# Four transformer layers between two graph convolutions: the ends of a layer rearranged

## The reference

```python
h = _gcn(batch_norm(relu(layernorm(x))), src, dst, gcn_in_w, gcn_in_b, n)
for i in range(L):                                  # L = 4
    a = _attn(_ln(h, ln2_w[i], ln2_b[i]), cond, Wq[i], Wk[i], Wv[i], Wo[i])
    h = h + a
    u = _ln(h, ln3_w[i], ln3_b[i]) @ geglu_w[i] + geglu_b[i]
    val, gate = jnp.split(u, 2, axis=-1)
    f = val * jax.nn.gelu(gate, approximate=False)
    h = h + f @ ffo_w[i] + ffo_b[i]
h = _gcn(h, src, dst, gcn_out_w, gcn_out_b, n)
return h + x_in
```

## Time and profile before

| | |
|---|---|
| median of 3 executions | 2628.73 us (2624.0 to 2635.95) |
| the profiled execution | 2636.97 us, its span 2635.2 us |
| mean granted clock of PE | 0.971 |
| PE busy | 2516.3 us, 95% of the span |
| DVE, ACT, POOL busy | 52%, 38%, 25% |
| first convolution | to 252 us |
| layers 1 to 4 | from 251.6, 828.4, 1405.2 and 1982 us, some 576.8 us each (windows; the last to 2557) |
| second convolution | the last 78 us |
| chain that ended last | PE 87%, DVE 7%, ACT 2%, issue 2% |
| loads of `stage` | 138 pieces of 512 KB, 3.3 us to landing; 32 cond groups of 1 MB, 4.8 us |

### The profile page before, as it was taken

How to read it: one execution, slowest core, us unless ns; L and a number is a source line. 1 busy time by engine, 2 the same in 40 slices (tenths; PEclk the granted TensorE clock), 3 DMA queues, 4 the chain that set the end, 5 groups by cost and what they waited for, 6 DMA issues and landing times.

```text
span 2635.2 us, 35448 instructions
## 1 busy us (share of the span) xinstructions
PE 2516.3 (95%) x12535; PEld 2077.5 (79%) x12535; DVE 1378.5 (52%) x2834; ACT 1002.0 (38%) x1956; POOL 648.7 (25%) x492
## 2 busy tenths in 40 slices
PE   5868999999999999999999999999999999999999
PEld 2517788888887888888887888888887888888877
DVE  8996676642224667632225676622235676522235
ACT  8524444352222433452222444442223434532230
POOL 3000000044442000154441000254440000254431
PEclk7879999999999999999999999999999999999999
DMA  2002000012120000011110000021110000021120
GB/s 104 1 16 100 33 33 16 33 41 73 64 68 33 33 32 32 17 65 65 66 65 34 32 17 32 33 65 64 64 63 23 33 32 32 17 80 64 65 99 33
DMA packets 30658, 123.05 MB, mean 47 GB/s; under 512 B 3136, under 2 KB 3520, under 8 KB 26048
## 3 DMA queue, kind: packets, MB, share of 16 engines
q1 hardware_dynamic: 30528, 121.36, 13.4%
HBM read 115.05 MB, written 6.29 MB: 46 GB/s over the span
## 4 chain that ended last, share of the span: by engine, by line
PE 87%; DVE 7%; ACT 2%; issue 2%; POOL 1%; DMA 1%; POOLq 0%; DVEq 0%; ACTq 0%; SPq 0%
PE ps L1377 26%; PE ps L1378 26%; PE ps L1379 26%; PE ps L1559 2%; PE ps L1576 2%; PE ps L1578 2%; PE ps L1573 1%; DVE oh_d L1068 1%; DVE oh_s L1066 1%; DVE z L1274 1%; PE ps L1600 1%; PE ps L1586 1%; ACT oh_d L613 1%; PE ps L1481 0%; PE ps L1614 0%
## 5 line engine op out<-in xcount | busy, mean ns | idle before, releaser
L1377 PE MATMUL ps<-xT_hi,wg_hi 128*128 128x512 f32 (+1 forms) x1088 | 416.8, 383 | 0.0
L1379 PE MATMUL ps<-xT_hi,wg_lo 128*128 128x512 f32 (+1 forms) x1088 | 415.1, 382 | 0.0
L1378 PE MATMUL ps<-xT_lo,wg_hi 128*128 128x512 f32 (+1 forms) x1088 | 414.9, 381 | 0.0
L1327 DVE SCALAR_TENSOR_TENSOR ff<-ps,cols_sb,gel 128x512 f32<-128x512 f32 x128 | 96.1, 751 | 593.9 <-ACT gel L823 593.9
L823 ACT ACTIVATE gel<-ps,cols_sb 128x512 f32<-128x512 f32 x128 | 88.2, 689 | 638.0 <-PE ps L1379 638.0
L1336 DVE TENSOR_TENSOR h<-h,ps 128x512 f32<-128x512 f32 x256 | 175.2, 687 | 139.8 <-PE ps L1379 139.8
L1378 PEld LDWEIGHTS ps<-xT_lo,wg_hi 128*128 128x128 f32 x1088 | 209.8, 193 | 37.5
L1379 PEld LDWEIGHTS ps<-xT_hi,wg_lo 128*128 128x128 f32 x1088 | 209.9, 193 | 37.3
L1377 PEld LDWEIGHTS ps<-xT_hi,wg_hi 128*128 128x128 f32 x1088 | 210.0, 193 | 37.1
L400 POOL TENSOR_SCALAR veps<-mv 128x1 f32<-128x1 f32 x64 | 14.0, 219 | 819.1 <-DVE mv L889 819.1
L1377 PE MATMUL ps<-w_hi,cond_hi 128*128 128x512 f32 x512 | 204.0, 398 | 8.2 <-DVE cond_lo L998 6.9
(11 more groups left out here) (240 smaller groups left out, 5414.2 us busy)
## 6 DMA issues: line engine op xcount, KB each, us to landing
stage<-in_pieces SPq DMA_DIRECT2D x138, 512.0 KB, 3.3
stage<-in_condT SPq DMA_DIRECT2D x32, 1024.0 KB, 4.8
x<-in_x SPq DMA_DIRECT2D x2, 1024.0 KB, 6.7
res_s<-x SPq DMA_DIRECT2D x2, 1024.0 KB, 4.2
at_s<-at SPq DMA_DIRECT2D x1, 2048.0 KB, 9.9
at16b<-at_s SPq DMA_DIRECT2D x1, 2048.0 KB, 7.6
out<-h SPq DMA_DIRECT2D x8, 256.0 KB, 2.0
bias_row<-in_rows SPq DMA_DIRECT2D x6, 256.0 KB, 3.6
```

Source lines behind the costliest of these rows:

```text
L1327: dve.scalar_tensor_tensor(ff[:, s % 2, :], ps[:, step_bank(j, a, s, 0), :], cols_sb[:, bass.ds(COL["geglu_b"] + 32 * l + 4 * j + 2 * a + ...
L1377: pe.matmul(bank, l_hi, r_hi, start=(first and i == 0), stop=False)
L1378: pe.matmul(bank, l_hi, r_lo, start=False, stop=False)
L1379: end = pe.matmul(bank, l_lo, r_hi, start=False, stop=(last and i == n - 1))
```

## The change

What moves, by place:

- **Statistics and z2 of a layer's first tile** are made at the end of the layer before (the statistics after the second of the last eight additions to h, z2 after the last), before DVE's branch. z2 goes to a place of its own, `z2_first` (over `o_full`). For the first layer both stand inside and after the first convolution's `gcn(0)`.
- **cond group 1** is loaded right after cond group 0, at the end of the layer before, and split at the very beginning of a layer: ACT and DVE do it before anything else there.
- **First products** on PE: V 0, t2, V 1, Q, K 0, Q's transposes, V 2, S 0; the fourth V product goes into unit 0. x2's low part of group 0 is made by DVE.
- **Weight parts.** The low parts of the MLP's first two pieces go from POOL to DVE, behind unit 1's and inside unit 2's work of the last group.
- **Bias row.** The eight additions of the bias row to h leave `z3_of` and stand before the second, third and fourth ff of the MLP (2, 3 and 3 tiles).
- **Last transposes.** t3(7) stands one half-width product later. x3's low part of tile 7 goes to DVE; POOL's are done in two halves.
- Smaller: PE enters the first layer after three tiles of h instead of eight (`gcn_ok`), ACT waits for `agg_mm` before its loop.

```diff
@@ -332,10 +334,12 @@
+            sp.wait_ge(c_lo, 2)
+            load_raw(1)
...
             with sp.Fori(0, L) as l:
-                with sp.Fori(1, GROUPS) as g:
+                with sp.Fori(2, GROUPS) as g:
@@ -354,6 +358,8 @@
                 load_raw(0)
+                wait_apart(sp, c_lo, 2 * GROUPS * l + 2 * GROUPS + 2)
+                load_raw(1)
@@ -459,8 +466,6 @@
-                rsqrt(norm0)
-                x2_low(0)
@@ -472,9 +477,11 @@
                     pool.wait_ge(x3_hi_ok, NT * l + t + 1)
-                    pool.tensor_tensor(xT3_lo[t // 4][:, :, r],
-                                       full[:, t % 2, :].rearrange("p (k n) -> p k n", n=P),
-                                       bits(xT3_hi[t // 4][:, :, r]), ALU.subtract).then_inc(x3_ok, 1)
+                    for ks in (slice(0, 2), slice(2, KC)):
+                        last = pool.tensor_tensor(xT3_lo[t // 4][:, ks, r],
+                                                  full[:, t % 2, :].rearrange("p (k n) -> p k n", n=P)[:, ks, :],
+                                                  bits(xT3_hi[t // 4][:, ks, r]), ALU.subtract)
+                    last.then_inc(x3_ok, 1)
@@ -500,15 +507,11 @@
                 x3_low(1)
-                for r in range(2):
-                    w_low(FIRST_PIECES + PIECES * l + r, r, up_place(0, 0, r), up_place(1, 0, r))
-                    if r == 0:
-                        rsqrt(norm0 + 2 * NT - 2)
+                rsqrt(norm0 + 2 * NT - 2)
...
                 weights_low(0, 0, 0)
-                x3_low(7)
@@ -522,6 +525,7 @@
                 zero_q()
+                rsqrt(norm0 + 2 * NT)
@@ -794,20 +799,19 @@
-                for mc in range(2):
-                    v_high(UNITS * l + mc, mc, 0, V_BANK + mc)
-                x2_high(GROUPS * l)
-                v_high(UNITS * l + 2, 2, 0, V_BANK + 2)
-                k_high(UNITS * l)
-                q_copy(GROUPS * l)
-                act.wait_ge(qb_zero, 2 * l + 2)
-                q_high(GROUPS * l)
-                v_high(UNITS * l + 3, 3, 0, V_BANK + 3)
-                unit(UNITS * l, GROUPS * l, 0, 0, first=True)
...
                     cond_high(1, 1, part, stage)
+                v_high(UNITS * l, 0, 0, V_BANK)
+                x2_high(GROUPS * l)
+                v_high(UNITS * l + 1, 1, 0, V_BANK + 1)
+                q_copy(GROUPS * l)
+                k_high(UNITS * l)
+                act.wait_ge(qb_zero, 2 * l + 2)
+                q_high(GROUPS * l)
+                v_high(UNITS * l + 2, 2, 0, V_BANK + 2)
+                unit(UNITS * l, GROUPS * l, 0, 0, first=True)
@@ -1154,6 +1158,9 @@
                                              ALU.mult, ALU.add).then_inc(gcn_ok, 1)
+                    if not use and t == 1:
+                        dve.wait_ge(gcn_ok, 1)
+                        norm_stats(0, [h[:, 0, :]])
@@ -1162,8 +1169,15 @@
+            def z2_of(g, k, place=z2):
+                norm_wait(k)
+                dve.tensor_scalar(place[:, :], h[:, g, :], mv[:, 0:1], rstd[:, 0:1],
+                                  ALU.subtract, ALU.mult).then_inc(z2_ok, 1)
...
             dve.wait_ge(gcn_ok, NT)
+            z2_of(0, 0, z2_first)
@@ -1244,12 +1258,14 @@
                         o_part(u - 1, (p + 3) % 4)
-                    if not (last and p >= 1 or first):
+                    if not (last and p >= 1):
...
                         o_low(g - 1)
+                    if p == 2 and last:
+                        up_low(1)
                     if ln2:
-                        z2_of(t + 1, 1 if first else 2 * t)
+                        z2_of(t + 1, norm0 + (1 if first else 2 * t))
@@ -1260,6 +1276,8 @@
                         x2_full(g + 1)
+                    if p == 1 and last:
+                        up_low(0)
@@ -1273,13 +1291,32 @@
                                       ALU.subtract, ALU.mult).then_inc(z3_ok, 1)
-                    dve.wait_ge(z3_ok, GROUPS * l + g + 1)
-                    dve.tensor_tensor(h[:, g, :], h[:, g, :], bias_row[:, :], ALU.add).then_inc(h_bias, 1)
-                def z2_of(g, k):
-                    norm_wait(norm0 + k)
-                    dve.tensor_scalar(z2[:, :], h[:, g, :], mv[:, 0:1], rstd[:, 0:1],
-                                      ALU.subtract, ALU.mult).then_inc(z2_ok, 1)
+                def add_bias(tiles):
+                    for t in tiles:
+                        dve.tensor_tensor(h[:, t, :], h[:, t, :], bias_row[:, :], ALU.add).then_inc(h_bias, 1)
+                def up_low(r):
+                    n = FIRST_PIECES + PIECES * l + r
+                    wait_apart(dve, w_hi_ok, n + 1)
+                    dve.tensor_tensor(up_place(1, 0, r), stage[:, r, :], bits(up_place(0, 0, r)), ALU.subtract)\
+                        .then_inc(w_ok, 1)
+                def x2_low(g):
+                    dve.wait_ge(x2_hi_ok, g + 1)
+                    dve.tensor_tensor(xT2_lo[:, :, :].rearrange("p k n -> p (k n)"), full[:, 0, :],
+                                      bits(xT2_hi[:, :, :].rearrange("p k n -> p (k n)")),
+                                      ALU.subtract).then_inc(x2_ok, 1)
+                def x3_low(t):
+                    r = slice(t % 4 * P, (t % 4 + 1) * P)
+                    wait_apart(dve, x3_hi_ok, NT * l + t + 1)
+                    wait_apart(dve, x3_ok, 2 + NT * l + t)
+                    dve.tensor_tensor(xT3_lo[t // 4][:, :, r], full[:, t % 2, :].rearrange("p (k n) -> p k n", n=P),
+                                      bits(xT3_hi[t // 4][:, :, r]), ALU.subtract).then_inc(x3_ok, 1)
@@ -1295,21 +1332,17 @@
-                norm_stats(norm0, [h[:, 0, :]])
-                z2_of(0, 0)
-                for mc in range(2):
-                    v_low(UNITS * l + mc, mc, 0, V_BANK + mc)
+                for part in range(2):
+                    cond_low(GROUPS * l + 1, 1, part, stage)
                 x2_full(GROUPS * l)
-                v_low(UNITS * l + 2, 2, 0, V_BANK + 2)
+                v_low(UNITS * l, 0, 0, V_BANK)
+                x2_low(GROUPS * l)
+                v_low(UNITS * l + 1, 1, 0, V_BANK + 1)
...
                 q_low(GROUPS * l)
-                v_low(UNITS * l + 3, 3, 0, V_BANK + 3)
+                v_low(UNITS * l + 2, 2, 0, V_BANK + 2)
...
                 unit(UNITS * l, GROUPS * l, 0, 0, first=True)
-                for part in range(2):
-                    cond_low(GROUPS * l + 1, 1, part, stage)
-                dve.wait_ge(row_in, 16 * l + 32)
@@ -1329,18 +1362,27 @@
-                def mlp_add(j, a):
+                def mlp_add(j, a, last=False):
...
                             .then_inc(h_ffo, 1)
+                        if last and t == 1:
+                            wait_apart(dve, h_ffo, 64 * l + 64 - NT + 1)
+                            norm_stats(norm0 + 2 * NT, [h[:, 0, :]])
...
                 mlp_step(0, 0, 0)
+                x3_low(NT - 1)
+                dve.wait_ge(row_in, 16 * l + 32)
+                dve.wait_ge(z3_ok, GROUPS * l + GROUPS)
+                add_bias(range(0, 2))
                 mlp_step(0, 0, 1)
+                add_bias(range(2, 5))
                 mlp_step(0, 0, 2)
+                add_bias(range(5, NT))
@@ -1354,8 +1396,9 @@
                     cond_low(GROUPS * l + GROUPS, 0, part, stage)
-                mlp_add(MG // 2 - 1, 1)
-                dve.wait_ge(h_ffo, 64 * l + 64)
+                mlp_add(MG // 2 - 1, 1, last=True)
+                wait_apart(dve, h_ffo, 64 * l + 64)
+                z2_of(0, norm0 + 2 * NT, z2_first)
@@ -1693,16 +1736,15 @@
-                for mc in range(2):
-                    v_product(None, mc, 0, V_BANK + mc)
-                t2(GROUPS * l)
+                v_product(None, 0, 0, V_BANK)
+                t2(GROUPS * l, z2_first)
+                v_product(None, 1, 0, V_BANK + 1)
+                q_product(GROUPS * l, first=True)
+                k_product(UNITS * l, 0, 0)
+                q_transpose(GROUPS * l)
                 v_product(None, 2, 0, V_BANK + 2)
-                k_product(UNITS * l, 0, 0)
-                q_product(GROUPS * l, first=True)
-                q_transpose(GROUPS * l)
-                v_product(None, 3, 0, V_BANK + 3)
-                pe.wait_ge(v_ok, UNITS * l + 3)
+                pe.wait_ge(v_ok, UNITS * l + 2)
@@ -1738,10 +1780,10 @@
                 mlp_product(0, 0, 1, 1).then_inc(u_mm, 1)
-                t3(7)
...
                 mlp_product(0, 0, 2, 0, slice(0, 2 * P))
+                t3(7)
...
                 mlp_product(0, 0, 2, 1, slice(0, 2 * P))
```

13 lines of the change are left out of this document (8 added, 5 removed).

## The result

The changed kernel takes **2641.17 us** (median of 5 runs, 2641.07 to 2643.37), the kernel before 2628.87 beside it (5 runs, 2624.0 to 2635.95): a ratio of 1.0048, 95% interval 1.0034 to 1.0062. The forecast was 2635 in a range of 2609 to 2648, no change within 0.5%: the ratio lies inside that, but the kernel is slower beyond doubt and the interval reaches past 0.5%. Execution against execution the sum was closer than the medians make it look: the profiled execution takes 2642.53 (span 2640.7), 5.6 above the 2636.97 of before, where the sum said 6.4. The kernel before spreads over 14 us: 64 runs of it, taken beside the kernels of this study, lie between 2624 and 2638 and their batches' medians between 2628.9 and 2636.6; the five executions of the changed kernel stay within 2.3. I had taken the whole 8.2 us between the profiled execution and the median of three off the forecast.

The account below looks back on a forecast made before the run. TensorE's own queue was taken as the bound, leaving only its idle time and slow clock to gain. Terms 3.5 + 2.8 + 3.2 - 9.2 - 6.7 = -6.4 gave 2643.4 us profiled, 2635 as a median, range 2609 to 2648.

Parts of the forecast that it names:

- Layers 2 to 4, beginning: Start of layers 2 to 4: old waits replaced by a 2.9 us wait before the Q product; 2.8 us gained.
- Rival (a): VectorE's gap is no part of the branch: Q product waits 0.5 us in layers 2 to 4; 2623 us, chance 0.08.
- First layer: First layer's beginning: idle time falls from 4.27 to 0.75 us, no clock counted; 3.5 us gained.
- two copies of 1.0 us: First layer: ScalarE splits cond group 1 after the aggregation in two copies of 1.0 us; TensorE then waits 0.5 us.
- Seam, first wait: pT wait gone, new 2.9 us wait for the second weight part; 4 x 0.8 = 3.2 us gained, bounds 0 and 7.6.
- I take 0.8, between them: First seam wait, gain per layer: 1.9 us with one slow clock stretch, 0 with two; 0.8 taken.
- Seam, second wait: Bias additions held beside POOL make ff(1) late: step 3 1.45 us later plus 0.85 clock per layer; 9.2 us lost.
- Last stage: End of last layer: at16b's load queues behind an unread cond load, 5.9 us later plus 0.8 clock; 6.7 lost.
- moved down by 8.2 at the end: Sum made against the profiled 2636.97 us, then lowered by its 8.2 us distance above the median of 2628.73.
- (b): Weight parts are in time, so the first seam wait and its clock go: 25.6 instead of 3.2; 2613 us, chance 0.08.
- (c): All four places, both seam waits and the layers' beginnings, come clear: 55.8 us gained, 2573 us, chance 0.12.
- (d): Bias additions also make ff(2), ff(3) late: one 2.4 us weight part more per layer, 9.6 in all; 2645 us, chance 0.20.

Follow-up runs that it names:

- the clean edit: Changed kernel with SP's body of the last layer written apart, without the load of cond group 1 that nothing reads: 2636.96 us.
- the gate on POOL: Changed kernel with the two first weight parts back on POOL, the second waiting until z3 of tile 6 is written: 2621.29 us.
- two gates in the old program: Kernel before the change with two waits on POOL: second weight part and wf's low part wait for the bias row on tiles 6 and 7: 2608.57 us.

## Why the prediction was right

The class, the range and the net of the profiled execution (5.6, forecast 6.4) are right, the class narrowly, and the net partly by luck: of its terms the last stage came as worked out, and at the beginnings and in the seams errors of both signs cancelled. In the order of the prediction:

- **Layers 2 to 4, beginning.** Gained 5.2 us, forecast 2.8. Wait, gap and order came as worked out (3.30 us, forecast 2.9; idle time of layer 3 from 4.3 to 3.4 us; clock loss 1.7 us before and after). The idle time falls by 2.5 us in the three layers; the forecast's own rows give 12.1 and not 12.4 for the idle time before, and so 2.5 too. Another 0.8 to 1.0 per layer lies in time that the profile counts as busy. Its cause I have not found; the clock it is not, as the first layer has 0.8 of it at full clock in both kernels. Rival (a) is out: the gap is the branch's.
- **First layer.** Gained 1.9, forecast 3.5. The step that failed is "two copies of 1.0 us": the wait was 1.99 and not 0.5, as the trace has a table load of 1.28 before them, which had been hidden and now stands on the path. Besides, 1.24 of the 3.5, the wait for the last h, lies ahead of the first mark. It is gone, but the first V product starts at 252.81 against 252.86: the waits within the first convolution differ by more from profile to profile (that product starts between 251.9 and 253.2 in the kernels with this beginning), so that part of the term is neither shown nor refuted. The 0.8 of busy time, which nobody forecast, hides a part of the miss.
- **Seam, first wait.** Forecast 3.2 gained, of which nothing came: from the first z3 to the first full-width product it is 34.84, 34.37, 34.62 and 34.76 us, against 34.57, 34.52, 34.57 and 34.60. The mechanism held (no pT wait, the second part waited for instead), the wait was 3.6 and not 2.9, as p_norm took 1.31 instead of 0.62 beside POOL; the half-width product came 0.7 us earlier in its layer's frame and not 1.56. The step that failed besides is "I take 0.8, between them": the slow clock behind the wait was as long as before (3.4 us lost in both), the prediction's case of two slow stretches, and took the 0.7 back. In the first layer, with 4.3 us of wait, the 0.7 did not come either. Where other kernels with this wait have half of that loss in layers 2 to 4 (1.7 us, one slow stretch), that part is 0.8 to 1.1 us shorter than before and not 1.9.
- **Seam, second wait.** From there to step 3 it is 1.45 us longer per layer, 5.8 in all, forecast 9.2. The 1.45 of the instructions is exactly what had been worked out (additions held, ff(1) late; ff(1) ends 20.5 us behind the first full-width product, as forecast); the 0.85 of clock put on top did not come, and the slow stretch of before is gone too. The run with the additions moved confirms the mechanism. These two errors, 3.5 (3.2 forecast as gained, 0.3 lost) and 3.4 us, cancelled: that the seams came out at 6.1 against 6.0 is luck.
- **Last stage.** 6.4 us longer, forecast 6.7; by the clean edit 6.2 of it is the load alone. at16b goes out 3.7 us later in its layer's frame (forecast 3.5) and takes 2.05 longer (2.4).
- **The median.** The step that failed is "moved down by 8.2 at the end": the kernel before has faster executions that one profile of it did not show, and the changed kernel has none of them in its five. Against all runs of before the difference lies between 4.6 us (batch median 2636.6) and 12.3 (2628.9), around the 6.4 of the sum.
- **Rivals.** (b) and (c) needed the second weight part in time; the gate on POOL shows that this was to be had, and that it is worth 21 us on the changed kernel. (d), additions so late that ff(2) and ff(3) are waited for too, did not happen: the only ff wait is the first.

## What to carry to other kernels

When an instruction that a late wait hangs on is held by another engine's, try first to order the two with a wait, before moving the work to the other engine: two gates in the old program gave 28 us at the seams, the rearrangement lost 6. A step moved to the head of a queue is paid for by everything behind it, so put first what the bound engine wants first. Before a sum leans on a wait removed, say where the clock goes after it: a shorter wait alone may give nothing back until its neighbours are gone as well.

## What the runs showed of the hardware

- A VectorE instruction with one tensor input in SBUF was held beside POOL as one with two is: z3 (one tensor, two columns) takes 2.50 us instead of 0.55, two p_norm 1.31 instead of 0.62, a bias addition (two tensors) 2.3 instead of 0.69. The Trainium skill, SBUF — State Buffer, section Who interferes with whom, has this for two tensors in SBUF and for VectorE's two-port modes, whoever issues first holding the shared ports to its end; whether z3 and p_norm ran in such a mode no row shows. The trace agrees on the order: POOL's 1.29 us became 2.28 where VectorE's weight part was issued first, and VectorE's 1.22 became 1.75 where POOL was. The maxima, which read PSUM, took 0.68 in the middle of POOL's weight part (1685.01 in the gated run), as always.
- A branch back of VectorE's loop costs 2.6 to 3.2 us in this program (3.2, 3.0 and 3.0 before, 2.8, 2.6 and 2.6 after), with one packet of instructions in it, over within 0.5 us; the first entry and the unrolled loop have none.
- Removing idle time did not always remove the slow clock. With 1.2 us per layer less idle (two waits for three) a stretch at 0.85 came and the total stayed; with a wait of 3.6 us gone the slow stretch moved to the next wait in two layers of four. Behind the same single wait of 1.9 us the clock stayed full in four layers of one kernel and fell in two of four in the next: the length of a wait alone did not decide it here.
- The kernel before has mean granted clocks of 0.972 to 0.979 over the span, at 2637.0 us and 2624.5 us: the same program, 0.5% apart.
